# Blank tails issued four experts at a time, and fixed TensorE products at the seams between the stages, in a gated cross-attention and mixture-of-experts kernel

## The chip, the cores and the metric

The kernel is one program on one core of a Trainium2 chip. The metric is the device time of one execution in microseconds. Three runs of the kernel before gave 1041.34, 1044.93 and 1046.5 us, so the median is 1044.93 us.

## What is computed

The input x is 32 sequences of 256 tokens with 256 features, 8192 tokens in all. There are two residual steps, each gated by the tanh of a scalar.

```python
x = x + tanh(g_xattn) * xattn(layernorm(x), ctx)      # 8 heads of 64; ctx: 77 rows of 192 per sequence
x = x + tanh(g_ffn) * ffn(layernorm(x))

def ffn(xf):
    scores = softmax(xf @ Wg.T)                       # 16 experts
    wk, idx = top_k(scores, 2)
    cw = sum(one_hot(idx, 16) * wk[..., None], axis=1)
    h = gated_mlp_act(einsum('td,edh->teh', xf, W1))  # u * silu(g), 128 wide
    z = einsum('te,teh,ehd->td', cw, h, W2)
    return z + gated_mlp_act(xf @ Ws1) @ Ws2          # shared expert, 256 wide
```

## The kernel before

The work is four stages, one after the other. Each of the functions `prepare`, `attend`, `mix` and `passes` opens one block; a block ends for all engines together, when the last of them has come to its end, and the next opens then. Every float32 operand of a large product is split into a high and a low part in the type float32r, and three products (high-high, low-high, high-low; lines 75 to 77) stand for one.

`prepare` (line 284) loads and splits the weights, folds the query weights and the keys of the first four sequences into matrices M, and gathers layer-norm statistics of all 64 tiles of x on VectorE. The last key product on TensorE is that of `make_K` in line 385; VectorE closes the block with the steps of `rstd_steps` (lines 105 to 131).

`attend` (line 455) goes over the 32 sequences: scores, softmax, values, output projection, and the first residual, stored to a scratch tensor x1. It leaves the statistics of the second layer norm in `c.stats2`, a tile of 128 partitions and 384 columns that stays in place through the rest of the program. So does `c.ident`, the 128x128 identity.

`mix` (line 796) goes over 16 steps of 512 tokens: it normalises the rows, transposes them on TensorE (`transpose_y`, line 970), computes the router's logits (`score`), the shared expert, the two best experts of each token and the slot of each token in two lists sorted by expert, one for each choice. POOL scatters the rows to the DRAM tensor rows1, in the order of the experts of one choice. At the end four products (line 1045) bring a table into PSUM, from which the program reads where each tile of slots lies and which expert's weights it needs.

An expert's list seldom ends with a whole tile of 128 rows. `blank_tails` (line 1277) therefore writes 128 blank rows behind the last row of each expert, sixteen DMAs of 258 KB for each choice, issued on SyncE's queue; their places are loaded into SyncE's registers four at a time (line 1283). A blank row carries an index that makes a later scatter skip it.

`passes` (line 1289) goes over 40 pairs of tiles twice: the first pass reads rows1 and scatters to rows0, the second reads rows0 and scatters to the output. Its order is written out by hand:

- SyncE loads the rows of pair q into one of ten buffers (`load`, line 1335), two DMAs of 258 KB, and before that waits until the pair ten places earlier has been scattered from the same buffer. Between the loads of pairs 10 and 11 of the first pass it issues all sixteen blank tails of rows0 (line 1349). Before the second pass it waits for all scatters of the first and for the tails.
- TensorE does four things in each step (line 1429): the transposes of pair q, the up product of pair q-1 (`hidden`), the transposes of the activations of pair q-2, the down product of pair q-3. The weights of all experts lie in SBUF.
- ScalarE and VectorE take the results out of PSUM, VectorE adds the result to the row in place (line 1500), and POOL scatters the two tiles of a pair by indirect DMA (line 1364).

The places that the tails fill and the rows that the scatters write do not overlap.

Of the kernel before, what the change touches and what calls it, by code (L numbers as in the profile page):

```python
# [33 lines left out]
E, HID = 16, 128  # L34
# [201 lines left out]
def make_K(nc, pe, c, a, n, pair):  # L236
    wait(pe, a.M_lo, 4 * n)
    out, cols = a.ps_proj[1][:, 0:GK], slice(pair * P, (pair + 1) * P)
    products(nc, out, [(c.wk_hi[:, 0, cols], c.wk_lo[:, 0, cols], a.ctxM[0][:, 0, :], a.ctxM[1][:, :])], stop=False)
    stacked(nc, out, c.wk_hi[:, 1, cols], c.wk_lo[:, 1, cols], a.ctxM[0][:, 1, :]).then_inc(a.K_done, 1)  # L240
# [40 lines left out]
    low(nc, M_out(a, 1, parity, cc, h), M_out(a, 0, parity, cc, h), M_bank(a, cc), a.M_lo)  # L281


def prepare(nc, c, a):


# [2 lines left out]
    with ExitStack() as ctx:  # L289
        sb, _, sem = allocator(nc, ctx)  # L290
# [24 lines left out]
        with nc.Block() as block:  # L315
# [59 lines left out]
            @block.tensor  # L375
            def _(pe):
                pe.wait_ge(wk_lo_done, 1)
                pe.wait_ge(a.ctx_split, 1)
                for n in range(4):
                    make_K(nc, pe, c, a, n, n)  # L380
                    pe.wait_ge(wq_lo_done, 2)
                    for k in range(4):
                        make_M(nc, pe, c, a, n, n, k)
                pe.wait_ge(a.ctx_split, 2)
                make_K(nc, pe, c, a, 4, 0)

            @block.scalar
            def _(act):
# [407 lines left out]
def mix(nc, c):  # L796
# [6 lines left out]
    with ExitStack() as ctx:  # L803
# [11 lines left out]
        a = [sb(f"ca{i}", [P, 512]) for i in range(2)]  # L815
# [57 lines left out]
        with nc.Block() as block:  # L873
# [95 lines left out]
            def _(pe):  # L969
# [44 lines left out]
                def down(G):  # L1014
                    p = G % 2
                    pe.wait_ge(aT_lo, 2 * G + 2)
                    for b in range(2):
# [4 lines left out]
                                 ws2[0][:, n, :], ws2[1][:, n, :]) for n in range(2)])  # L1022
                        last.then_inc(o_done, 1)

                transpose_y(0)
                pe.wait_ge(wg_ready, 1)
                score(0)
# [17 lines left out]
                for n, column in enumerate((1, 0, 3, 2)):  # L1045
                    last = nc.tensor.matmul(ps_table[:, n * SLOT_TILES:(n + 1) * SLOT_TILES],
                                            table[0:SLOT_TILES, column:column + 1], c.ident[0:SLOT_TILES, 0:SLOT_TILES],
                                            start=True, stop=True)
                last.then_inc(table_rows, 1)

            @block.scalar
            def _(act):
# [236 lines left out]
def passes(nc, c):  # L1289
# [5 lines left out]
    with ExitStack() as ctx:  # L1295
# [35 lines left out]
        with nc.Block() as block:  # L1331

            @block.sync
            def _(sp):
                def load(dram, q):
                    u = q % U
                    wait(sp, scattered[u], 32 * (q // U))
                    with ExitStack() as registers:
                        held = [registers.enter_context(sp.register(f"rows_{q}_{i}")) for i in range(2)]
                        first = 2 * q  # L1340
                        sp.load(held, c.rows_at[0:1, first:first + 2])  # L1341
                        for i in range(2):
                            at = sp.snap(held[i], donate=True, min_val=0, max_val=ROWS - P)
                            sp.dma_start(row[u][:, i, :], dram[bass.ds(at, P), :]).then_inc(row_in[u], 16)  # L1344

                sp.wait_ge(c.blanked1, 16 * E)
                for q in range(PAIRS):
                    load(c.rows1, q)
                    if q == U:
                        blank_tails(nc, sp, nc.sync, c, c.rows0, 0, range(E), c.blanked0)  # L1350
                for u in range(U):
                    sp.wait_ge(scattered[u], 32 * ROUNDS)
                sp.wait_ge(c.blanked0, 16 * E)
                for q in range(PAIRS, 2 * PAIRS):
                    load(c.rows0, q)
# [21 lines left out]
            @block.tensor  # L1377
            def _(pe):


                def transpose_rows(q, u, j):
                    pe.wait_ge(row_in[u], 32 * (j + 1))
                    wait(pe, yT_lo, q - 1)
                    for i in range(2):
                        for k in range(DC):
                            last = nc.tensor.transpose(ps_y[u % 2][:, k, i * P:(i + 1) * P],  # L1386
                                                       row[u][:, i, YROW + k * P:YROW + (k + 1) * P], c.ident[:, :])
                    last.then_inc(yT_done, 1)

                def split(at, first):  # L1390

                    return (c.w_flat[:, bass.ds(at + first, D)], c.w_flat[:, bass.ds(at + (WHALF + first), D)])

                def hidden(q, p, at):
                    pe.wait_ge(yT_lo, q + 1)
                    wait(pe, a_done, 2 * (q - 1))
                    for i in range(2):
                        token = slice(i * P, (i + 1) * P)
                        last = products(nc, ps_h[p][:, i, :], [
                            (yT[p][0][:, k, token], yT[p][1][:, k, token], *split(at[i], k * D)) for k in range(DC)])  # L1400
                    last.then_inc(h_done, 1)

                def transpose_a(q, p):
                    pe.wait_ge(a_done, 2 * q + 2)
                    wait(pe, aT_lo, q - 1)
                    for i in range(2):
                        last = nc.tensor.transpose(ps_a[p][:, i, :], a[p][:, i, :], c.ident[:, :])  # L1407
                    last.then_inc(aT_done, 1)

                def down(q, p, at):  # L1410
                    pe.wait_ge(aT_lo, q + 1)
                    wait(pe, final, q - 1)
                    for i in range(2):
                        last = products(nc, ps_z[p][:, i, :], [
                            (aT[p][0][:, i, :], aT[p][1][:, i, :], *split(at[i], DC * D))])
                    last.then_inc(z_done, 1)

                def load_weights_at(known, q, u):


                    _, at = nc.values_load_multi_w_load_instructions(
                        c.weights_at[0:1, bass.ds(2 * q + 2, 4)], engines=[mybir.EngineType.PE], min_val=0,
                        max_val=(E - 1) * WROW, skip_runtime_bounds_check_because="the table is made of min(., E - 1)")
                    known[u], known[u + 1] = at[0:2], at[2:4]

                for first in (0, ROUNDS):
                    exists, known = inside(first), {}

                    def step(s, u, j):
                        if u == 0:  # L1430
                            known.clear()
                            if exists(s - 3):
                                load_weights_at(known, s - 3, -3)
                        if u % 2 == 0:
                            load_weights_at(known, s - 1, u - 1)
                        if exists(s):
                            transpose_rows(s, u, j)
                        if exists(s - 1):
                            hidden(s - 1, (u - 1) % 2, known[u - 1])
                        if exists(s - 2):  # L1440
                            transpose_a(s - 2, u % 2)
                        if exists(s - 3):
                            down(s - 3, (u - 3) % 2, known[u - 3])

                    rounds(pe, step, first, lag=3)
# [140 lines left out]
```

## Time and profile before

| | before |
|---|---|
| median of three runs | 1044.93 us |
| the profiled execution: its own time | 1043.86 us |
| its span in the trace | 1041.7 us |
| TensorE products, busy | 909.5 us (87%) |
| TensorE weight loads, busy | 857.2 us (82%) |
| VectorE, busy | 804.5 us (77%) |
| ScalarE, busy | 478.8 us (46%) |
| POOL, busy | 475.1 us (46%) |
| DMA traffic | 150.64 MB, mean 145 GB/s |
| mean granted TensorE clock | 0.956 of full speed |

The profile is that of one execution. Its page gives the busy time of each engine, and then the span in 40 slices of 26 us: a digit is the busy share of a slice in tenths, and the row of the clock gives the TensorE clock that was granted, 9 standing for 0.9 and more. The program's stages lie one after the other in these slices: `prepare` ends at 62 us, `attend` at 530, `mix` at 760; the second pass of `passes` begins near 908. [...] Before its first change in a trace the clock is printed as 1.00 whatever it is, so there the length of the products tells it.

### The profile page before, as it was taken

To read this page: it belongs to the slowest core of one execution; us is meant where nothing else is said; L and a number is where in the kernel's file an instruction comes from. 1 tells how busy PE (TensorE), PEld (TensorE's weight loads), DVE (VectorE), ACT (ScalarE), POOL (GpSimd) and SP (SyncE) were. 2 spreads that over 40 slices of the span, in tenths; PEclk is the share of its full clock that TensorE was granted. 3 is DMA by queue.
4 is the path that set the end of the run, shared out by engine and by line. 5 is a ranking of instruction groups with operands and counts; after the bars stand their busy time and mean duration, and the time that the engine had idled before them with its cause. 6 is when DMAs were issued, how large, how long until landed. Compare 5 with 4: busy or idle time off the path is not lost. (4 is left out here: it accounts for less than half of the span.)

```text
span 1041.7 us, 22369 instructions
## 1 busy us (share of the span) xinstructions
PE 909.5 (87%) x6728; PEld 857.2 (82%) x6729; DVE 804.5 (77%) x1837; ACT 478.8 (46%) x970; POOL 475.1 (46%) x495
## 2 busy tenths in 40 slices
PE   2559999999999999999949999999565899599994
PEld 2449999999999999998847888887465899499994
DVE  5768888888898888998737898888534677467773
ACT  3345555555555555554445455543122344144441
POOL 6134434343343434334321555455415466537775
PEclk9999999999999999999968999999868899889998
DMA  8621222122221222212151444442769899488890
GB/s 216 215 87 35 80 68 67 54 57 79 66 79 45 66 66 67 68 54 67 53 172 32 173 166 160 170 170 108 275 222 318 284 341 344 146 267 260 268 289 29
DMA packets 108096, 150.64 MB, mean 145 GB/s; under 512 B 21622, under 2 KB 72186, under 8 KB 108032
## 3 DMA queue, kind: packets, MB, share of 16 engines
q1 hardware_dynamic: 92672, 107.60, 34.1%
q0 software_dynamic: 15360, 42.24, 10.6%
q8 instruction: 35, 0.57, 0.2%
q14 instruction: 29, 0.24, 0.1%
HBM read 90.19 MB, written 65.90 MB: 150 GB/s over the span
## 5 line engine op out<-in xcount | busy, mean ns | idle before, releaser
L549 POOL TENSOR_TENSOR prob<-prob,row_sum 128x616 f32<-128x616 f32 x64 | 77.9, 1218 | 148.7 <-DVE row_sum L739 148.7
L1364 POOL DMA_INDIRECT rows_scratch<-prow x80 | 78.7, 983 | 75.0 <-DVE prow L1500 47.2
L956 POOL DMA_INDIRECT rows_scratch<-row,slot x64 | 67.8, 1060 | 75.8 <-DVE row L1203 61.2
L1364 POOL DMA_INDIRECT out<-prow x80 | 78.7, 983 | 50.1 <-issue 26.4
L1482 DVE TENSOR_TENSOR eyT_lo<-ps_ey,eyT_hi 128x512 fp32r<-128x512 f32 x80 | 55.2, 690 | 55.6 <-ACT eyT_hi L1457 55.1
L1457 ACT ACTIVATE eyT_hi<-ps_ey 128x512 fp32r<-128x512 f32 x80 | 47.9, 599 | 109.3 <-PE ps_ey L1386 109.3
L75 PE MATMUL ps_h<-w_flat,eyT_hi 128*128 x320 | 98.1, 307 | 0.0
L224 POOL TENSOR_TENSOR xT_lo<-xT_raw,xT_hi 128x512 fp32r<-128x512 f32 x32 | 41.2, 1286 | 121.7 <-ACT ctxb_hi L190 121.6
L1386 PE MATMUL ps_ey<-ident,prow 128*128 128x128 f32 x320 | 51.6, 286 | 49.2 <-DMA prow<-rows_scratch 45.9
L190 ACT ACTIVATE M_hi<-ps_proj 128x308 f32 (+1 forms) x128 | 54.4, 429 | 84.1 <-PE ps_proj L77 84.0
L76 PE MATMUL ps_h<-w_flat,eyT_hi 128*128 x320 | 90.9, 284 | 0.0
L77 PE MATMUL ps_h<-w_flat,eyT_lo 128*128 x320 | 90.7, 283 | 0.0
L75 PE MATMUL ps_s<-M_hi,xT_hi 128*128 (+1 forms) x256 | 81.4, 318 | 8.7 <-PEq L315 8.5
L1489 DVE SCALAR_TENSOR_TENSOR a<-ps_h,prow,silu 128x128 f32<-128x128 f32 x160 | 48.8, 347 | 47.8 <-ACT silu L1462 47.8
L195 DVE TENSOR_TENSOR PT_lo<-ps_pt,PT_hi 77x512 fp32r<-77x512 f32 x128 | 80.9, 671 | 0.3 <-ACT PT_hi L190 0.3
L1386 PEld LDWEIGHTS ps_ey<-ident,prow 128*128 128x128 f32 x320 | 38.5, 147 | 51.7 <-DMA prow<-rows_scratch 47.3
L76 PE MATMUL ps_s<-M_lo,xT_hi 128*128 (+1 forms) x256 | 78.6, 307 | 0.0
L77 PE MATMUL ps_s<-M_hi,xT_lo 128*128 (+1 forms) x256 | 78.6, 307 | 0.0
L75 PE MATMUL ps_o<-wo_hi,OT_hi 128*128 128x256 f32 x256 | 74.6, 291 | 1.4 <-DVE OT_lo L195 1.4
L75 PE MATMUL ps_o<-PT_hi,V_hi 96*128 96x256 f32 x256 | 72.9, 285 | 3.3 <-DVE PT_lo L195 3.3
L675 ACT ACTIVATE prob<-prob,rstd 128x616 f32<-128x616 f32 x64 | 52.0, 812 | 44.8 <-DVE prob L729 44.8
L76 PE MATMUL ps_o<-PT_lo,V_hi 96*128 96x256 f32 x256 | 72.4, 283 | 0.0
(232 smaller groups left out, 3383.3 us busy)
## 6 DMA issues: line engine op xcount, KB each, us to landing
prow<-rows_scratch SPq DMA_DIRECT2D x160, 258.0 KB, 3.8
rows_scratch<-blank SPq DMA_DIRECT2D x34, 258.0 KB, 4.0
xs<-in_x SPq DMA_DIRECT2D x16, 512.0 KB, 4.5
xT_raw<-in_xT SPq DMA_DIRECT2D x32, 256.0 KB, 3.8
x_tok<-in_x SPq DMA_DIRECT2D x32, 256.0 KB, 2.9
x_scratch<-x_tok SPq DMA_DIRECT2D x32, 256.0 KB, 3.0
row<-x_scratch SPq DMA_DIRECT2D x16, 512.0 KB, 4.0
w_raw<-in_W SPq DMA_DIRECT2D x16, 256.0 KB, 3.5
```

The lines of the kernel that those rows point to most:

```text
L75: nc.tensor.matmul(out, lh, rh, start=start and n == 0, stop=False)
L76: nc.tensor.matmul(out, lh, rl, start=False, stop=False)
L77: last = nc.tensor.matmul(out, ll, rh, start=False, stop=stop and n == len(pairs) - 1)
L190: nc.scalar.activation(out, source, ACT.Copy).then_inc(done, 1)
L195: nc.vector.tensor_tensor(lo, source, f32(hi), ALU.subtract).then_inc(done, 1)
L549: nc.gpsimd.tensor_tensor(pr, pr, row_sum[i][:, :].unsqueeze(2).broadcast_to((P, H, CK)), ALU.mult).then_inc(normed, 1)
L675: nc.scalar.activation(prob[i][:, :], prob[i][:, :], ACT.Exp, scale=c.rstd1[:, bass.ds(2 * b + i, 1)]).then_inc(exp_done, 1)
L956: pool.indirect_dma_start(c.rows1, bass.IndirectOffsetOnAxis(slot1[:, t:t + 1], 0), row[G % NX][:, i, :], None).then_inc(scattered[G % NX] ...
L1364: pool.indirect_dma_start(dram, bass.IndirectOffsetOnAxis(target, 0), row[u][:, i, 0:columns], None, bounds_check=bound, oob_is_err=False) ...
L1386: last = nc.tensor.transpose(ps_y[u % 2][:, k, i * P:(i + 1) * P], row[u][:, i, YROW + k * P:YROW + (k + 1) * P], c.ident[:, :])
L1482: V.tensor_tensor(yT[p][1][:, :, :], ps_y[p][:, :, :], f32(yT[p][0][:, :, :]), ALU.subtract).then_inc(yT_lo, 1)
L1489: V.scalar_tensor_tensor(a[p][:, i, :], ps_h[p][:, i, 0:HID], row[b][:, i, weight:weight + 1], silu[p][:, i, :], ALU.mult, ALU.mult).then_ ...
```

## The change

Four edits. After the last key product of `prepare`, TensorE does 24 products of the identity with itself. In `mix` it does ten products of the identity with the 384 columns of `c.stats2` ahead of the first transposes, and eighteen behind the table's products. In `passes` it does four such products at the opening of the first pass and eighteen ahead of the second. All are plain float32, go to a PSUM bank that is free at the time, wait for nothing, signal nothing and are read by nobody. And SyncE issues the blank tails of rows0 in groups of four experts, behind the loads of pairs 10, 16, 22 and 28, in place of all sixteen behind the load of pair 10.

```diff
@@ -281,6 +281,12 @@
     low(nc, M_out(a, 1, parity, cc, h), M_out(a, 0, parity, cc, h), M_bank(a, cc), a.M_lo)
 
 
+def busy(nc, c, bank, operand, count):
+
+    for _ in range(count):
+        nc.tensor.matmul(bank[:, 0:operand.shape[1]], c.ident[:, :], operand, start=True, stop=True)
+
+
 def prepare(nc, c, a):
 
 
@@ -383,6 +389,7 @@
                         make_M(nc, pe, c, a, n, n, k)
                 pe.wait_ge(a.ctx_split, 2)
                 make_K(nc, pe, c, a, 4, 0)
+                busy(nc, c, a.ps_proj[0], c.ident[:, :], 24)
 
             @block.scalar
             def _(act):
@@ -1022,6 +1029,7 @@
                                  ws2[0][:, n, :], ws2[1][:, n, :]) for n in range(2)])
                         last.then_inc(o_done, 1)
 
+                busy(nc, c, ps_h[0], c.stats2[:, :], 10)
                 transpose_y(0)
                 pe.wait_ge(wg_ready, 1)
                 score(0)
@@ -1047,6 +1055,7 @@
                                             table[0:SLOT_TILES, column:column + 1], c.ident[0:SLOT_TILES, 0:SLOT_TILES],
                                             start=True, stop=True)
                 last.then_inc(table_rows, 1)
+                busy(nc, c, ps_h[0], c.stats2[:, :], 18)
 
             @block.scalar
             def _(act):
@@ -1346,8 +1355,9 @@
                 sp.wait_ge(c.blanked1, 16 * E)
                 for q in range(PAIRS):
                     load(c.rows1, q)
-                    if q == U:
-                        blank_tails(nc, sp, nc.sync, c, c.rows0, 0, range(E), c.blanked0)
+                    first = (q - U) * 4 // 6
+                    if q >= U and (q - U) % 6 == 0 and first < E:
+                        blank_tails(nc, sp, nc.sync, c, c.rows0, 0, range(first, first + 4), c.blanked0)
                 for u in range(U):
                     sp.wait_ge(scattered[u], 32 * ROUNDS)
                 sp.wait_ge(c.blanked0, 16 * E)
@@ -1423,8 +1433,9 @@
                         max_val=(E - 1) * WROW, skip_runtime_bounds_check_because="the table is made of min(., E - 1)")
                     known[u], known[u + 1] = at[0:2], at[2:4]
 
-                for first in (0, ROUNDS):
+                for first, idle in ((0, 4), (ROUNDS, 18)):
                     exists, known = inside(first), {}
+                    busy(nc, c, ps_h[0][:, :, :].rearrange("p i h -> p (i h)"), c.stats2[:, :], idle)
 
                     def step(s, u, j):
                         if u == 0:
```

## Rows read from the trace of the kernel before

**Rows 1.** The page, part 2: TensorE's busy tenths and granted clock in 40 slices.
```profile
PE   2559999999999999999949999999565899599994
...
PEclk9999999999999999999968999999868899889998
```

**Rows 2.** Waits of TensorE from 764 to 1030 us: total, times, longest.
```profile
PE ps_ey L1386 <- DMA prow<-rows_scratch: 45.9, 5, 17.2
```

**Rows 3.** The chain that ended last, first pass: start, length (us), what.
```profile
784.07 0.31 SPq L1283
...
788.10 0.46 SPq L1283
...
810.46 1.12 PE ps_ey L1386 x4
...
814.73 0.44 PE ps_ey L1386 x4
...
848.92 0.44 PE ps_ey L1386 x4
...
851.67 0.44 PE ps_ey L1386 x4
```

**Rows 4.** Timeline of the first pass, SyncE's queue and one step of TensorE.
```profile
784.54 17.83 SPq L1286 DMA_DIRECT2D rows_scratch<-blank  x16
...
850.60 11.57 SPq L1344 DMA_DIRECT2D prow<-rows_scratch  x9
...
856.99 0.60 PE L1386 MATMUL ps_ey<-ident,prow 128*128 128x128 f32 x4
```

**Rows 5.** The page, part 6: DMA issues, median us to landing at the end.
```profile
prow<-rows_scratch SPq DMA_DIRECT2D x160, 258.0 KB, 3.8
```

**Rows 6.** Waits of SyncE's queue from 820 to 890 us: total, times, longest.
```profile
SPq L1341 <- DMA rows_scratch<-prow: 28.1, 20, 6.8
```

**Rows 7.** Windows of the first pass; last three columns: granted clock, DMA share, GB/s.
```profile
784.00:890.00 106.00, 88.94 (x761) 88.22 (x760) 69.61 (x160) 39.59 (x94) 62.24 (x64) 0.94 0.96 328
...
786.00:798.00 12.00, 9.29 (x80) 8.92 (x78) 8.22 (x19) 4.42 (x11) 7.86 (x8) 1.00 1.04 367
...
840.00:880.00 40.00, 39.16 (x342) 38.99 (x342) 30.73 (x71) 18.06 (x44) 27.04 (x28) 1.00 0.99 341
```

**Rows 8.** Timeline of TensorE at the passes' starts; brackets: idle before, its releaser.
```profile
746.29 0.71 PE L1046 MATMUL ps_r<-ident,table 80*1 80x80 f32 x8
...
764.20 1.11 PE L1386 MATMUL ps_ey<-ident,prow 128*128 128x128 f32 x4 [17.19 <-DMA prow<-rows_scratch]
...
767.04 0.56 PE L75 MATMUL ps_h<-w_flat,eyT_hi 128*128 x1
...
911.28 1.12 PE L1386 MATMUL ps_ey<-ident,prow 128*128 128x128 f32 x4 [12.37 <-DMA prow<-rows_scratch]
```

**Rows 9.** Timeline from the end of `prepare` into `attend`.
```profile
53.95 0.46 PE L85 MATMUL ps_proj<-ctxM_hi,wk_lo 128*128 128x308 f32 x1
...
62.95 0.60 PE L75 MATMUL ps_s<-M_hi,xT_hi 128*128 128x308 f32 x1 [8.54 <-PEq L315]
...
66.17 0.46 PE L75 MATMUL ps_proj<-kT_hi,wq_hi 128*128 128x308 f32 x1
...
69.23 0.30 PE L76 MATMUL ps_s<-M_lo,xT_hi 128*128 128x308 f32 x1
```

**Rows 10.** Timeline from the opening of `mix` to its first transposes.
```profile
530.84 0.27 DVE L117 TENSOR_TENSOR mean<-stats 128x64 f32<-128x64 f32 x1 [2.22 <-PEq L504]
...
538.32 1.97 PE L975 MATMUL ps_cy<-ident,row 128*128 128x128 f32 x8 [10.62 <-ACT row L1084]
```

**Rows 11.** The chain at the opening of `passes`: SyncE's first register load.
```profile
760.01 0.47 SPq L1341
```

**Rows 12.** Windows in which the clock rises again; columns as in rows 7.
```profile
772.00:774.00 2.00, 2.00 (x18) 2.00 (x17) 0.76 (x4) 1.01 (x3) 0.00 (x0) 0.93 1.03 322
...
918.00:920.00 2.00, 2.00 (x15) 2.00 (x15) 1.04 (x3) 0.60 (x1) 0.00 (x0) 0.73 1.01 346
```

## The prediction

> **What bounds the kernel now.** I read the page first. Its slices show a TensorE that is nine tenths busy nearly everywhere, with dips at four places, and at these places, or just behind them, the granted clock drops too [rows 1]. [...] Then the waits of TensorE alone over the expert passes: 45.9 us go to rows that had not landed, in five waits [rows 2]. Three are the starts of the two passes; one is inside the first pass, and the chain says why: SyncE issues a burst of blank tails (line 1286), and the eleventh pair's rows come behind it [rows 3]. Last the timeline at the four seams between stages, read below: they hold 8.54, 10.62, 17.19 and 12.37 us without a product.
>
> **The tails.** The sixteen DMAs take the queue from 784.54 to 802.37; TensorE has ten pairs of rows in hand, uses them up and stands still until 810.46. The step from pair to pair is 2.75 us in the steady state (848.92 to 851.67), so the pair that starts at 810.46 would have started 14.2 us earlier: the idle stretch, 14.15 us by the timeline, is lost whole. The next pair follows after 4.27 us (810.46 to 814.73, counted to its transposes) in place of 2.75, since the clock has fallen: another 1.5. The stall costs 15.7 us [rows 3, 4].
>
> What comes back? The change issues the same sixteen DMAs, four behind each of the loads 10, 16, 22 and 28. One group of four held SyncE for 4.0 us (784.07 to 788.10). In the steady state the ring has little to lend: the ninefold issue row begins at 850.60 with the load that TensorE uses at 856.99; landing takes 3.8 us in the median from the issue of the second half some 0.5 us later, so 2 us are spare [rows 4, 5]. SyncE itself waits for scatters (28.1 us in 20 waits over 25 pairs), 1.1 us per pair, and can catch up in that [rows 6]. By the queue alone the first group is free (six or more us in hand there), and each later one costs 0 to 2 us: 0 to 6.
>
> The DMA engines are the harder limit. From 784 to 890 they moved 328 GB/s over 106 us, 34.8 MB, and all of it stays. With 15.7 us less they would have to carry 34.8 MB in 90.3 us, 385 GB/s. The steady stretch moves 341 at a busy share of 0.99, the crowded 786 to 798 moves 367 at 1.04 [rows 7]. At 341 GB/s the stretch takes 102.0 us, which gives back 11.7; at 367 it takes 94.8 and gives back 4.5; at 385 nothing. I take 6 us, near the row with all three kinds of transfer in it, which is the mix that the change makes. Net of the tails: 15.7 - 6 = 9.7 us, bounds 4 and 15.7. [...]
>
> **The fixed products.** Each is an identity times 128 or 384 columns of plain float32. The nearest row is the table product of line 1046: four calls are eight records of 80 columns, and the eight start within 0.48 us (0.71 less the last's 0.23), 0.069 apart [rows 8]. [...] A call of 384 columns is then 0.64 us at the full clock and 1.28 at half, one of 128 columns 0.21 and 0.43. None signals anybody; each delays only what follows on TensorE, and the end of its block.
>
> Seam A (24 of 128 columns): from 54.4, where the last key product ends, to 62.95, where attention opens after VectorE's chain [rows 9]. 5.1 us at full clock, 10.2 at half. The products run at half clock until 69.2 (the first one of 0.30 us in place of 0.46 is at 69.23), 6.2 us after dense work begins; if the burst raises the clock as this dense work did, it needs at most 6.2 + 2 = 8.2 us and ends in time. Gain: the twelve score products that open the stage, 62.95 to 66.17, shrink by 1.6 us, and the softmax chain that the first transposes wait for starts that much earlier. Taken 1.5; bounds 2 late and 3 early.
>
> Seam B (10 of 384): the block opens at 530.8, rows are ready for transposes at 538.32 [rows 10]. 6.4 us at full clock, 12.8 at half; the clock is low at the start, so 8 to 10 us, which ends 0.5 to 2.5 us late. It then speeds the transposes and the scores behind them, and the clock may drop in the waits between. Taken 1; bounds -3 and 3.
>
> Seam C (18 behind the tables, 4 at the opening of the passes): from 747.0, the clock being full, 11.5 us to 758.5; SyncE's first load of the passes is at 760.01, so the block's end isn't delayed; four more take 2.6 us and end ahead of the rows at 764.20. Without them the clock stayed low until the slice 772 to 774 (0.93), some 8 us, 5 of them dense; that is worth 2.6 us at most [rows 8, 11, 12]. A quiet stretch before the rows come lets the clock fall again, so I take 1.5; bounds -2 and 3.
>
> Seam D (18): 898.9 + 11.5 = 910.4, just ahead of 911.28. The low clock lasted into the slice 918 to 920 (0.73): again 1.5, bounds -1 and 3 [rows 8, 12].
>
> **Sum.** 9.7 + 1.5 + 1 + 1.5 + 1.5 = 15.2 us. The profiled execution took 1043.86 us (span 1041.7 and 2.2 around it); 1028.7 by it. The median of the runs is 1.1 us above that execution: 1029.8, said as 1029.5.
>
> **The rivals.**
> R1, the engines have room: short stretches carry the 385 GB/s. Nothing comes back, 15.7, and the seams give 5.5 to 8: 1021 to 1024. For it speaks that shares above 1 occur; against, the steady rows at 0.99 with 341. 0.12.
> R2, the seams give nothing: the wait for rows behind each burst drops the clock again before dense work begins. For it: at C and D the first pair's transposes stand alone for 2 us before the second pair lands. [...] As a mechanism here it takes B, C and D to zero and leaves A: 9.7 + 1.5, so 1033.7. 0.18.
> R3, the tails' stall is split, not removed: each group holds the queue its 4.0 us with no slack left, 16 us for four against 15.7. Only the seams count: about 1039.5. Against it are the 2 us in the ring and SyncE's own idle time. 0.12.
> R4, slower: plain float32 identity products do not keep or raise the clock. Then the bursts run at half clock: A 10.2 us ends at 64.6 (1.7 late), B 12.8 at 543.6 (5.3 late), C 23 at 770.0 and the four on top at 775 (11 late), D 23 at 921.9 (10.6 late), 28.6 late in all; less 9.7, 19 us slower, 1064. It decides from the point where C and D run at half clock for over 5 us each. Against it: at C and D the clock is full when the burst begins. 0.07.
>
> **How the numbers follow.** Forecast 0.51, R1 0.12, R2 0.18, R3 0.12, R4 0.07. The range 1021 to 1039 holds the first three and half of R3. About 0.5% (5 us) is what a measurement of this kernel can tell from no change, the runs before spread by as much; so below 1039.7 is faster: forecast, R1, R2 and half of R3, 0.87. The other half of R3 is the same, 0.06, and R4 slower, 0.07.
>
> **What would show it.** No wait of 14 us inside the first pass; in its place a few of 1 to 3 us behind loads 16, 22 and 28, each with a line 1286 ahead of it, and the DMA share at 1.0 until the pass ends. The first pass's steady step still 2.75. Fixed products 0.64 us apart at C and D with the granted clock at 1.00 between 747 and 759. The score products at 63 to 66 some 0.13 apart, not 0.26. I am wrong if the stretch of the pass is shorter by under 5 or over 14 us, or if a seam's first real product comes more than 2 us later than now.

## The result

The changed kernel takes **1039.16 us** (median of six runs, 1034.72 to 1041.35) against 1045.89 of the kernel before in the same comparison (six runs, 1041.34 to 1047.29). The ratio is 0.9933, 95% interval 0.9906 to 0.996: 6.7 us faster, between 4.2 and 9.8. The forecast was 15.2 us faster, so more than half of the gain isn't there. The profiled execution took 1040.25 us, 3.6 less than that of before; what is read between the two traces below has to add up to 3.6, and can't account for the other 3 us of the medians.

The page of the kernel after, TensorE's busy tenths, its clock and the DMA engines' busy tenths in 40 slices, then the landing time of rows; to be held against [rows 1] and [rows 5]:

```profile
PE   2579999999999999999968999999889789999994
PEclk9989999999999999999998999999999898999997
DMA  7631221222221222112142444443869999388890
...
prow<-rows_scratch SPq DMA_DIRECT2D x160, 258.0 KB, 3.8
```

The dips of TensorE at the seams are mostly filled, as they must be: the fixed products count as busy. In the first pass the clock shows two dips (slices 32 and 34) in place of the one long dip of [rows 1] (slices 31 and 32). That is the place to look. TensorE's waits for rows from 784 to 890 us in the kernel after (total, times, longest):

```profile
PE ps_ey L1396 <- DMA prow<-rows_scratch: 11.2, 4, 4.9
```

In the kernel before it was one wait of 14.15 us. So nothing of 14 us is left, as foretold, but four waits hold 11.2 us, and the clock makes up the rest. The timeline of TensorE around the second of them, with the transposes of six pairs in turn:

```profile
806.38 0.60 PE L1396 MATMUL ps_ey<-ident,prow 128*128 128x128 f32 x4
809.13 0.60 PE L1396 MATMUL ps_ey<-ident,prow 128*128 128x128 f32 x4
816.92 1.11 PE L1396 MATMUL ps_ey<-ident,prow 128*128 128x128 f32 x4 [4.89 <-DMA prow<-rows_scratch]
822.10 0.87 PE L1396 MATMUL ps_ey<-ident,prow 128*128 128x128 f32 x4
825.12 0.60 PE L1396 MATMUL ps_ey<-ident,prow 128*128 128x128 f32 x4
```

The steps are 2.75, 7.79, 5.18 and 3.02 us. After an idle stretch of only 4.89 us the transposes take 1.11 in place of 0.60, and the step behind it is almost double: the granted clock, 1.00 before, is 0.50 from 815.8 to 822.7. (All the clock records of the twenty traces of this case read 1.00 or 0.50; what lies between is the mean of a window. That is the "full" and "half" of the prediction.) That costs 2.4 us on top of the wait. The fourth group brings the same again: a wait of 4.28 us at 858.17, the clock at 0.50 from 856.8 to 863.6, then a step of 5.19. Windows of the kernel after (PE, PEld, VectorE, ScalarE, GpSimd busy, then granted clock, DMA share, GB/s):

```profile
784.00:887.00 103.00, 90.84 (x739) 89.57 (x738) 67.95 (x155) 38.83 (x93) 60.71 (x62) 0.93 0.96 334
...
792.00:804.00 12.00, 10.22 (x90) 9.90 (x88) 7.78 (x19) 4.43 (x11) 6.80 (x7) 1.00 1.04 391
812.00:817.00 5.00, 0.11 (x2) 0.08 (x2) 1.18 (x3) 0.00 (x0) 3.26 (x4) 0.88 1.04 401
817.00:823.00 6.00, 6.00 (x30) 6.00 (x31) 2.30 (x5) 1.33 (x3) 0.00 (x0) 0.53 1.03 374
866.00:872.00 6.00, 6.00 (x55) 6.00 (x54) 4.83 (x12) 2.76 (x7) 3.94 (x5) 1.00 0.68 201
```

While TensorE stands still (812 to 817) the DMA engines are full, a share of 1.04 at 401 GB/s: the rows that it waits for are issued and under way. Later the engines run part empty (866 to 872, 0.68): a load waits for the scatter of the pair that held its buffer, and TensorE has fallen behind with that pair. SyncE's waits from 862 to 876 us:

```profile
SPq L1350 <- DMA rows_scratch<-prow: 8.8, 3, 4.0
```

So the high rates of a few microseconds aren't kept: over 103 us it is 334 GB/s.

What a group of four can do shows in the chain that ended last, in the kernel after, at the second group:

```profile
801.15 0.31 SPq L1292
...
801.97 0.36 SPq L1295
...
803.92 1.02 SPq L1295
...
805.00 1.11 SPq L1350
...
806.27 0.35 SPq L1353
...
806.81 10.07 DMA prow<-rows_scratch
816.92 1.11 PE ps_ey L1396 x4
```

From the register load (line 1292) to the next load of rows (line 1353) the group holds SyncE about 5 us, of which some 2.5 are a delay: the last packet of the scatter that freed the buffer landed at 802.9. Then the rows take 10.07 us to land, counted from the issue of the pair's second half. The 3.8 us of [rows 5] is no measure for that: it is a median over both passes. Where the trace tells the landing of a load, it took, in the kernel before from 784 to 890 us and from 914 to the end, and in the kernel after from 784 to 890:

```profile
DMA to landing us min/median/max: 3.7/4.6/6.3
DMA to landing us min/median/max: 2.6/3.4/4.3
DMA to landing us min/median/max: 3.2/5.5/7.0
```

Without tails in the stretch (e5 below) the second halves alone take 5.0 us in the median. Against that the landing at this group is 5 us late and the queue 2.5; at the fourth group (7.87 us to land, the buffer free at 843.9, the load issued at 849.7) it is nearly 3 us each. Both have a share, and the landing's is not the smaller one.

To compare stages I use the starts of the transposes of pairs 0, 4, 10, 39 and 40, and like marks at the other stages (us, one profiled execution each; "e7" and the like are experiments below). "Attention" goes from its first score product to the last product ahead of `mix`.

| stretch | before | after | e7 tails alone | e8 products alone | e5 tails last | e6 last + products |
|---|---|---|---|---|---|---|
| start to first score product | 62.9 | 64.3 | 63.2 | 64.2 | 63.3 | 63.7 |
| attention | 464.8 | 466.6 | 464.7 | 465.6 | 465.6 | 466.3 |
| its end to first transposes of `mix` | 10.6 | 10.6 | 10.8 | 12.5 | 10.6 | 12.6 |
| from there to the end of the table product | 208.7 | 205.0 | 208.6 | 206.0 | 208.7 | 206.1 |
| from there to pair 0 | 17.2 | 17.6 | 17.7 | 17.2 | 17.7 | 17.2 |
| pair 0 to pair 4 | 11.5 | 9.2 | 11.1 | 10.3 | 11.2 | 10.2 |
| pair 4 to pair 10 | 17.6 | 17.1 | 17.4 | 17.3 | 16.9 | 17.1 |
| **pair 10 to pair 39** | **97.7** | **97.7** | **95.7** | **100.0** | **83.7** | **83.3** |
| pair 39 to pair 40 | 20.2 | 20.2 | 20.3 | 20.7 | 21.2 | 22.0 |
| pair 40 to the end of TensorE's last product | 116.4 | 115.8 | 115.5 | 115.6 | 116.4 | 115.5 |

The bold row is where the tails stand, and it hasn't moved at all. 29 steps of 2.75 us would be 79.8; both kernels lose 18 us there. Between these two traces the gain of 3.6 us comes from `mix` (3.7) and the opening of the first pass (2.3), with half a microsecond each from pairs 4 to 10 and from the second pass, less what the start of attention, attention itself and the way to pair 0 lose (3.6). The rows ahead of the passes have to be read with care: over the twenty traces of this case attention takes 464.1 to 468.1 us, 464.1 to 466.6 in the six with products ahead of it and 464.7 to 468.1 in the fourteen without, so that the 1.8 us that it "loses" here tell nothing.

### The profile page after: what moved, and what is told of

The parts are those of the page before. It is cut to its first block and busy times, and to the rows that moved or that the text cites. A ratio compares the mean times of both kernels' runs of the same rounds, so it can differ in the third digit from the quotient of the medians.

```text
span 1038.1 us, 22665 instructions
## 1 busy us (share of the span) xinstructions
PE 945.8 (91%) x6876; PEld 879.8 (85%) x6877; DVE 803.0 (77%) x1837; ACT 479.2 (46%) x970; POOL 475.6 (46%) x495
## 5 line engine op out<-in xcount | busy, mean ns | idle before, releaser
L963 POOL DMA_INDIRECT rows_scratch<-row,slot x64 | 67.8, 1059 | 76.5 <-DVE row L1212 61.8
L77 PE MATMUL ps_o<-PT_hi,V_lo 96*128 96x256 f32 x256 | 73.0, 285 | 0.0
L76 PE MATMUL ps_o<-wo_lo,OT_hi 128*128 128x256 f32 x256 | 71.9, 281 | 0.0
```

What stands on the lines that cost most here:

```text
L76: nc.tensor.matmul(out, lh, rl, start=False, stop=False)
L77: last = nc.tensor.matmul(out, ll, rh, start=False, stop=stop and n == len(pairs) - 1)
L963: pool.indirect_dma_start(c.rows1, bass.IndirectOffsetOnAxis(slot1[:, t:t + 1], 0), row[G % NX][:, i, :], None).then_inc(scattered[G % NX] ...
```

## The experiments

Two theories of the measured gain at first: **A**, the stall comes back (the third rival), and what is gained are the seams; **B**, the tails give most of it and the seams nothing or less. For the stall there were in turn two causes: the **bytes** of the tails, which share full engines with the rows, or SyncE's **queue**, held by a register load and four issues. The kernel before is run beside every kernel; a ratio is to it, on the same chip.

### The halves, and the tails in another stage

e1: the kernel after without any fixed product. e2: only the products, the tails where the kernel before has them. e3: no products, and all sixteen tails moved ahead of the passes, behind the other sixteen in `mix`. e4: e3 with the products.

```diff
 e1, e3 (every call of busy goes)
-                busy(nc, c, ps_h[0], c.stats2[:, :], 18)
 e2
-                    first = (q - U) * 4 // 6
-                    if q >= U and (q - U) % 6 == 0 and first < E:
+                    if q == U:
-                        blank_tails(..., range(first, first + 4), c.blanked0)
+                        blank_tails(..., range(E), c.blanked0)
 e3, e4
                 blank_tails(nc, sp, nc.sync, c, c.rows1, 1, range(E), c.blanked1)
+                blank_tails(nc, sp, nc.sync, c, c.rows0, 0, range(E), c.blanked0)
```

> The tails in groups of four, no fixed products. Theory 1 (crowded ring: a group of four in DMA engines that are already full delays the rows behind it and the scatters beside it, and the ring of ten buffers has only some 2 us to lend): the first pass gains nothing clear, 0 to 3 us, so 1043 to 1046; two or three stalls of 2 to 5 us stay in the trace. Rival (the forecast's term of 9.7 us holds and the fixed products cost what is missing): 1035 to 1038.

> The fixed products, the sixteen tails in one piece as before. Theory 1: nearly the whole of the measured gain is theirs, 4 to 8 us, so 1038 to 1042, and the first pass keeps its one stall of 14 us. Rival: the products gain nothing or lose, 1044 to 1048.

> No fixed products, and the tails of the second pass issued in the stage before, right behind those of the first, where TensorE is idle and the DMA engines run empty from 754 on. Theory 1: the first pass runs without a stall at 2.75 us per pair, and the stage before ends no later, since its end waits for POOL's drain at 759.8: 15 to 17 us less, 1028 to 1031. Rival (the DMA engines cannot carry rows and scatters at that step either, so that stalls stay): 5 to 10 less. Second rival (the sixteen DMAs push the last scatters and the end of the stage back): 8 to 12 less, with the first load of the passes 4 us or more later.

> The tails as in the run before this one, with the fixed products of the change. If the two parts add up: the gain of the tails in the stage before plus that of the products alone, 1021 to 1025. If the products only win where a stall left the clock low: no better than the run without them.

Measured: e1 0.9947 (0.992 to 0.9974), e2 1.001 (0.9985 to 1.0035), e3 0.9983 (0.9961 to 1.0005), e4 0.9942 (0.992 to 0.9964). On this chip, though, the kernel before took 1104.5 us, 59 more than in the comparison that gave the result, so none of the times foretold can be held against it, and the traces show why the ratios can't be carried over either. Both passes go at about 3.6 us per pair in place of 2.75; the stages ahead of them are as long as ever. TensorE's waits in e18, a later run on such a chip, from 800 to 870 us:

```profile
PE ps_h L75 <- DVE eyT_lo L1489: 9.8, 8, 1.5
PE ps_ey L1392 <- issue: 3.4, 4, 1.6
```

It never waits for rows there, but for VectorE and its own instructions: ScalarE and VectorE both fall silent together, for 3.3 and 2.7 us, every 7.3 us or so (806 to 828). The DMA engines have room in such a pass, a share of 0.84 in e18 from 800 to 870, so it can't show what tails cost where rows are the limit.

It shows the other side, what fours do where there is room. From 784 to 900 us e1's share of the DMA engines is 0.92, and TensorE never waits for rows there. e2, with the sixteen in one piece, still has the stall (its waits from 784 to 905 us):

```profile
PE ps_ey L1395 <- DMA prow<-rows_scratch: 9.7, 1, 9.7
```

Its pairs 10 to 39 take 114.9 us, e1's 107.3; in the twelve traces of slower passes that have tails one by one, behind the last load or in `mix`, they take 102.9 to 107.1. So here the stall does go when it is split, as the forecast had it for the faster passes. (e2 has the fixed products and e1 not, but none of them stands in this stretch.) e4 is 5.0 us below e3 by the medians, with intervals that barely overlap, while the products of e2 give nothing.

e3 is no gain, for the reason that its second rival gave. SyncE's queue in e3:

```profile
733.00 27.36 SPq L1293 DMA_DIRECT2D rows_scratch<-blank  x32
766.23 5.49 SPq L1351 DMA_DIRECT2D prow<-rows_scratch  x8
```

Thirty-two tails hold it to 760.4. GpSimd's scatters of `mix` share the engines with them (a DMA share of 1.01 from 733 to 760, 0.74 in e1), its drain behind the last one starts at 760.04 in place of 755.81 (e1), and the first load of the passes goes out at 766.23 in place of 762.05. From the table product to pair 0 e3 takes 22.3 us, e1 17.3.

### Tails behind the last load, and the halves again

On a chip where the kernel before takes 1042.81 us (19 runs; e5 and e6 have four runs each, e7 and e8 ten). e5: no products; all sixteen tails behind the first pass's last load, when SyncE has nothing else to fetch. e6: e5 with the products. e7 and e8 are e1 and e2 again.

```diff
 e5, e6
                 for q in range(PAIRS):
                     load(c.rows1, q)
-                    first = (q - U) * 4 // 6
-                    if q >= U and (q - U) % 6 == 0 and first < E:
-                        blank_tails(..., range(first, first + 4), c.blanked0)
+                blank_tails(nc, sp, nc.sync, c, c.rows0, 0, range(E), c.blanked0)
```

> No fixed products; all sixteen tails behind the last load of the first pass, where SyncE has nothing to do for some 20 us and the DMA engines are half empty and then empty. Theory 1 (the tails' cost lies in delaying rows and scatters in full DMA engines): the first pass runs through at 2.75 us per pair with no wait for rows after the opening, its span shrinks by 15 to 17 us, and the second pass starts no later behind it: 1028 to 1031 where the kernel before takes 1044 to 1046. Rival (the DMA engines cannot carry rows and scatters alone at that step, so waits appear anyway): 5 to 10 us less only. On a chip of the kind of the first batch, where both passes run at some 3.6 us per pair, rows are no limit and the gain shrinks to 5 to 12.

> As the run before this one, with the change's fixed products. Theory 1 and products that give 2 to 6 us at the seams: 1023 to 1027. Rival (the products give nothing on top): within 1.5 us of the run without them.

> The change's tails in groups of four, no products, once more, in case the chip is one that runs the passes at 2.75 us per pair: theory 1: 0 to 4 us less than before (1041 to 1046), with two or three stalls in the first pass whose idle time and low clock together cost 12 to 18 us. Rival (forecast): 8 to 12 less.

> The fixed products, tails in one piece, once more. Theory 1: 3 to 6 us less than before (1039 to 1042). Rival, as the first batch had it: no difference, 0 to 1 us.

| kernel | median us | ratio | 95% |
|---|---|---|---|
| e5 | 1031.33 | 0.9886 | 0.9857 to 0.9915 |
| e6 | 1028.99 | 0.9853 | 0.9825 to 0.988 |
| e7 | 1039.82 | 0.9964 | 0.9949 to 0.998 |
| e8 | 1042.29 | 0.9998 | 0.9979 to 1.0017 |

e5 settles that the price of the tails lies in their standing inside the full stretch. From pair 10 to pair 39 it takes 83.7 us in place of 97.7: **14.0 us**, against the 15.7 that I had counted for the stall. On its own chip the same step out of the stretch is worth 12.0 us from fours (e7 to e5) and 16.7 from one piece (e8 to e6). By the medians e5 is 11.5 us below the kernel before, just above the 1028 to 1031 that was expected. TensorE's waits for rows in e5 from 784 to 890 us:

```profile
PE ps_ey L1391 <- DMA prow<-rows_scratch: 1.8, 2, 0.9
```

Its windows, columns as above:

```profile
784.00:876.00 92.00, 88.36 (x767) 87.51 (x767) 69.78 (x160) 40.10 (x96) 62.64 (x65) 1.00 0.97 332
872.00:890.00 18.00, 13.61 (x110) 12.59 (x108) 11.43 (x26) 5.05 (x13) 12.56 (x14) 0.98 1.04 368
```

And its queue:

```profile
784.39 87.22 SPq L1350 DMA_DIRECT2D prow<-rows_scratch  x60
872.12 17.69 SPq L1292 DMA_DIRECT2D rows_scratch<-blank  x16
895.43 3.97 SPq L1350 DMA_DIRECT2D prow<-rows_scratch  x6
```

The tails take SyncE 17.7 us, as in [rows 4], but now TensorE has the last ten pairs in hand. The price is 1.0 us at the change of passes (21.2 against 20.2). The clock stays at 1.00 until 876 and the engines' share at 0.97: without the tails the DMA engines are still nearly full, and the two waits of 1.8 us in all show how little is spare.

e7 says what spreading in fours does by itself: two waits, 8.3 us in all, where e5 has 1.8, and the step from pair 10 to pair 39 is only 2.0 us shorter than in the kernel before. Its chain ahead of the first of them:

```profile
795.96 5.76 DMA rows_scratch<-prow
801.74 0.95 SPq L1347
...
804.60 0.36 SPq L1292
...
809.03 0.35 SPq L1350
809.57 7.90 DMA prow<-rows_scratch
817.52 1.11 PE ps_ey L1393 x4
```

Here the load ahead of the group has to wait for a scatter (5.76 us), then comes the group, then a load that lands in 7.90. So the pattern of the kernel after isn't its products' doing. At the medians e7 is 3.0 us below the kernel before, inside the 0 to 4 of its theory. e8: the products alone are worth nothing that this can measure (0.9998, 2 us either way), as its rival had it, though the table shows 2.7 us won in `mix` and 1.2 at the opening of the first pass; 1.9 us of later first transposes, 2.1 of a later and longer attention, and a longer pass 10 to 39 (100.0, with the one stall of 15.2 us) stand against it in that trace. On top of e5 they bring 2.3 us more (e6), with intervals that overlap: not shown, and neither what its theory nor what its rival said. e6 is the fastest kernel seen here, 13.8 us below the kernel before by the medians, 15.3 by the ratio (12.5 to 18.2). That is about what I had forecast for the change, but by other sums: its tails give 11.5 where I had 9.7, its products 2.3 where I had 5.5.

So neither theory of the gain is shown. By the two profiled executions the seams gave all of it and the stretch nothing; by the halves on this chip the tails in fours gave 3.0 us (0.2 to 0.5%, clear of zero) and the products nothing clear. The halves together make less than the 6.7 us of the whole change on its own chip.

### Bytes or queue

e10: no products, the tails one at a time behind every second load from the eleventh pair's on. e11: tails behind the last load as in e5, but in the change's four places SyncE still loads four registers and issues four DMAs of 16 bytes a row to a place that nobody reads: the queue's time without the bytes. e9 and e12: e6 with the products only in `mix`'s end and the passes' openings, and e5 with only the 24 products that end `prepare`.

```diff
 e10
-                    first = (q - U) * 4 // 6
-                    if q >= U and (q - U) % 6 == 0 and first < E:
-                        blank_tails(..., range(first, first + 4), c.blanked0)
+                    first = (q - U) // 2 if q % 2 == 0 else E - 1
+                    if q >= U and (q % 2 == 0 or q == PAIRS - 1):
+                        blank_tails(..., range(first, first + 1), c.blanked0)
 e11
-                        blank_tails(..., range(first, first + 4), c.blanked0)
+                        narrow_blanks(nc, sp, c, c.nowhere, first, c.blanked0)
+                blank_tails(nc, sp, nc.sync, c, c.rows0, 0, range(E), c.blanked0)
...
+        eng.load(held, c.tails[0:1, first:first + 4])
+        for i in range(4):
+            nc.sync.dma_start(dram[at:at + P, 2 * D:ROW], c.blank[:, 2 * D:ROW]).then_inc(done, 16)
 e9 (of e6)
-                busy(nc, c, a.ps_proj[0], c.ident[:, :], 24)
...
-                busy(nc, c, ps_h[0], c.stats2[:, :], 10)
 e12 (of e5)
+                busy(nc, c, a.ps_proj[0], c.ident[:, :], 24)
```

> All tails behind the last load, and fixed products only around the passes (18 behind the tables, 4 and 18 at the passes' openings), none in the two earlier seams. If those two seams cost as much as they give (what the traces so far show: the attention stage not shorter, the transposes of the next stage 1.9 us late against 2.6 us gained behind them), this is no slower than tails last with all products, and 1.5 to 4 us faster than tails last alone: 1026 to 1030. Rival (the earlier seams give): 1 to 3 us slower than with all.

> No products; the sixteen tails inside the first pass one at a time, behind every second load from the tenth on. If what hurts is four in a row, each single tail (0.7 us of the DMA engines) is lent by the ring, and most of the 14 us that leaving the tails out of the pass gives is had: 1032 to 1036. Rival (the DMA engines are full, so the sixteen cost their own time wherever in the full stretch they stand, some 11 us): 1039 to 1043.

> Tails last, no products; in the change's four places SyncE loads four registers and issues four DMAs as there, but each writes 16 bytes a row in place of 2064, to a tensor that nobody reads. If the bytes in the full DMA engines are what stalls the pass: the time of tails last alone, within 2 us (1030 to 1033). If SyncE's time at the issue is (four DMAs and a register load, 2.5 to 4 us in front of the next load): the stalls come back, 6 to 12 us slower than tails last.

> All tails behind the last load, and only the 24 products at the end of the first stage. If they give nothing: within 1 us of tails last alone, the attention stage again 464.7 to 466.5 us long and opened 0.3 to 1 us later. Rival (my step A): 1 to 3 us faster than tails last alone.

The chip was again one of the slower passes (the kernel before 1099.8 us), so the questions that the expectations put were not answered: e9 0.992 (0.9891 to 0.995), e10 0.9939 (0.9914 to 0.9964), e11 0.9941 (0.9915 to 0.9967), e12 0.9955 (0.9928 to 0.9983). e10 and e11 differ from each other by nothing, and from e12 by nothing that the intervals part. e10, e11 and e9 were run twice more, for a chip on which rows are the limit (e13 and e16 are e10, e14 and e17 are e11, e15 and e18 are e9, without a changed line):

> One tail behind every second load, no products, once more, for a chip that runs the passes at 2.75 us per pair. If what hurts is four in a row: most of the 14 us, 1032 to 1036. Rival (the DMA engines are full, the sixteen cost their own 11 us wherever they stand in the full stretch): 1039 to 1043.

> Tails last, and in the change's four places register loads and DMAs of 16 bytes a row, once more. If the bytes stall the pass: within 2 us of tails last alone (1030 to 1033). If SyncE's time at the issue does: 6 to 12 us slower than tails last.

> Tails last, products only around the passes, once more. If the earlier two seams pay for nothing: 1027 to 1030, no slower than tails last with all products (1029.0 where the kernel before takes 1042.8). Rival: 1 to 3 us slower than that.

> One tail behind every second load, no products, a third time, since both tries fell on chips that run the passes at some 3.6 us per pair. At 2.75 us per pair: 1032 to 1036 if four in a row is what hurts, 1039 to 1043 if the sixteen cost their own time wherever they stand in the full stretch. At 3.6 us per pair: again 0.3 to 0.8% less than before, which tells nothing of the two.

> Tails last with narrow groups in the change's places, a third time. At 2.75 us per pair: within 2 us of tails last (1.1% less than before) if the bytes stall the pass; 0.2 to 0.6% less than before if SyncE's time at the issue does. At 3.6 us per pair: again 0.4 to 0.8% less than before.

> Tails last, products only around the passes, a third time. At 2.75 us per pair: 1.2 to 1.7% less than before if the two earlier seams pay for nothing, 1.0 to 1.2% if they give. At 3.6 us per pair: again 0.6 to 1.1% less.

| | first | second | third |
|---|---|---|---|
| kernel before, us | 1099.82 | 1104.08 | 1099.99 |
| one by one (e10, e13, e16) | 0.9939 | 0.9944 | 0.993 |
| narrow groups (e11, e14, e17) | 0.9941 | 0.994 | 0.9922 |
| last, products at the passes (e9, e15, e18) | 0.992 | 0.9913 | 0.993 |

Both times the slower passes came again. In a window of e11 where three of its groups fall, the DMA share is 0.87; the question needs it near 1. Columns as above:

```profile
800.00:870.00 70.00, 58.23 (x476) 54.91 (x475) 42.90 (x97) 23.36 (x58) 37.44 (x39) 1.00 0.87 272
```

All nine intervals end below 1 (the highest at 0.9967), so on such chips too each of the three is worth 0.6 to 0.9%; more these runs don't tell apart. **Bytes or queue stays open as an experiment.** What speaks for the bytes is the trace and a sum. At the second group a load that was late by 2.5 us in the queue took 5 us longer to land than such loads do in e5. And sixteen tails of 258 KB are 4.2 MB, 12.7 us at the 334 GB/s of the stretch, of the 14.0 us that e5 wins by taking them out of it. What speaks for the queue is that it was late by 2.5 to 3 us at each of the two groups that TensorE waited longest behind. Neither is proof.

## Why the prediction failed, step by step

**The reading of the stall was right.** I had 15.7 us for it, and e5, which takes the tails away from the full stretch, wins 14.0 us there and 11.5 at the median.

**"What comes back" is the step that failed.** Of the 15.7 us, 15.7 came back in the kernel after and 13.7 in e7, by the bold row; my own sign of being wrong, a stretch shorter by under 5 us, is there. I took 6 us, between 4.5 at 367 GB/s and 11.7 at 341, because the crowded 12 us of [rows 7] had the mix of transfers that the change makes. A rate over 12 us isn't one over 100. The kernel after does reach 391 and 401 in short windows; but each stall that they end in leaves the engines part empty later (201 GB/s from 866 to 872), since loads wait for scatters and those for TensorE. Over the stretch it is 334. In my own formula, 34.8 MB at 334 GB/s are 104.2 us, and of 15.7 come back 13.9; what's left is 1.8, and the two traces with the tails in fours show 0 and 2.0. That sum is bookkeeping, since the rate is read from the very stretch whose length it gives; it says that the formula was sound and its rate wrong, not why the rate is what it is. [Rows 7] had 328 GB/s over 106 us with the stall in it, at a share of 0.96 already; e5, which hardly waits for rows, has 332 at 0.97. The bound at the steady row was still too hopeful, and the middle was the wrong end.

**The queue's own bound was also too kind**, 0 to 6 us with 2 us spare. The slack was worked out with rows that land in 3.8 us, the median over both passes. In the very stretch the kernel before's landed in 4.6 in the median, which leaves 1 us spare and not 2, before any tail is added. Behind a group they landed in 10.07, 7.87 and 7.90 us, so the slack is gone before the queue's delay is counted. The first group I called free; a wait of 1.78 us stood behind it. I foretold "a few of 1 to 3 us", and got 4.89 and 4.28, with the clock at 0.50 behind both. That price I had charged to the one stall and not to its parts: 2.4 us each, 5 in all. These 5 and the 11.2 us of waits are the 16 us of the third rival. Its total, 1039.5, stands beside 1039.16, just outside the range (1021 to 1039); but that is partly luck, for it has the seams give 5.5 us, which they did not. Its mechanism was half right: at the two long waits the queue was late by 2.5 to 3 us, and the landing by 5 and 3.

**Prices of the products: right.** The fixed products behind the tables and before pass two, timeline of the kernel after:

```profile
746.51 11.88 PE L287 MATMUL ps_ch<-stats,ident 128*128 128x384 f32 x36
...
895.89 11.77 PE L287 MATMUL ps_h<-stats,ident 128*128 128x384 f32 x36
...
908.34 0.66 PE L1396 MATMUL ps_ey<-ident,prow 128*128 128x128 f32 x4 [0.68 <-DMA prow<-rows_scratch]
```

36 records in 11.88 us are 18 calls of 0.64 us (11.5) and the tail of the last, ending at 758.4 (758.5 was said) and 907.7. The granted clock was 1.00 from 746 to 759 and from 896 to 908, so no plain float32 product ran at half clock there. The row of 0.069 us for 80 columns would by proportion give 0.66 a call and not 0.64; what I reckoned with is what the runs show. A call is two records in the trace. One of 384 columns takes 0.32 us from start to start at a clock of 1.00 and 0.64 at 0.50 (e8, 533 to 538), so a call 0.64 and 1.28; one of 128 columns takes 0.21 before the clock's rise at 58.1 and 0.11 behind it in the kernel after, a call 0.43 and 0.21. The fourth rival is out.

**Seam A: wrong.** 1.5 us said, nothing gained. TensorE in the kernel after from the burst on:

```profile
55.80 5.94 PE L287 MATMUL ps_proj<-ident 128*128 128x128 f32 x42
64.33 0.38 PE L75 MATMUL ps_s<-M_hi,xT_hi 128*128 128x308 f32 x1 [2.60 <-PEq L321]
...
66.30 0.46 PE L75 MATMUL ps_s<-M_hi,xT_hi 128*128 128x308 f32 x1
...
69.53 0.31 PE L75 MATMUL ps_s<-M_hi,xT_hi 128*128 128x308 f32 x1
```

The burst raised the clock, in fact: it rose at 58.1 (first rise at 56.9 to 58.9 in the six traces with these products, at 66.4 to 69.6 in the fourteen without). The burst ended at 61.7, TensorE stood for 2.60 us, and half a microsecond after the stage opened, at 64.9, the clock fell to 0.50, until 68.3: the score products have 0.46 us each, as before. I had written that it "ends in time" and held the clock for won. That VectorE's chain, and with it attention, also starts later here (64.3 against 62.95; 64.2 in e8) was no part of my sum; over all traces that is 63.5 to 64.3 in the six with these products and 61.8 to 64.2 in the fourteen without, so a price of theirs is not shown.

**Seam B: right in kind, low in size.** Said 1 us. In `mix` the kernel after is 3.7 us shorter (2.7 in e8 and 2.6 in e6), and its products met the clock at 1.00 (534.2 to 540.2):

```profile
534.10 6.69 PE L287 MATMUL ps_ch<-stats,ident 128*128 128x384 f32 x20 [3.14 <-PEq L511]
541.56 1.09 PE L982 MATMUL ps_cy<-ident,row 128*128 128x128 f32 x8 [0.77 <-ACT row L1093]
```

In e8 and e6 it was not so: the clock was 0.50 until 538.7 and 539.0, the same burst took 9.57 and 9.61 us and the transposes came 1.9 and 2.0 later, as my "0.5 to 2.5" had it. The net is then under 1 us. The gain behind the transposes is real: from them to the end of the table product it is 205.0 to 206.3 us in the five traces with these products, and 207.3 to 209.0 in the fifteen without.

**Seam C: right.** 2.3 us from pair 0 to pair 4 (1.5 said), 1.2 in e8; the rows were there 1.24 us after the last product, and the clock was still at 1.00. Over all traces pairs 0 to 4 take 8.6 to 10.5 us with these products and 10.2 to 11.9 without. **Seam D:** 1.5 said, some 0.5 found (11.0 against 11.5 from pair 40 to 44). Here the second rival's mechanism has its place: waits of 0.68 and 2.01 us for rows follow the burst, and the clock was at 0.50 again from 911.4 to 914.8 in the kernel after. At seam C the waits were 1.24 and 1.76, and it stayed at 1.00; in e8 they were 1.32 and 1.45, and it was 0.50 from 767.4 to 770.8. In the slower passes seam D gave more: with the tails last, pairs 40 to 44 took 8.7 to 9.3 us (e9, e15, e18) against 11.4 without products (e12). Together the seams made between 0 (e8, medians) and 3 us (the profiled executions), not 5.5.

## What to carry to other kernels

DMAs that are spread through a stretch where the engines' busy share is already near 1 (0.96 in the kernels before and after) can cost there what they cost in one piece (97.7 us both ways here, 95.7 in e7); where there was room (0.92 in e1) the stall went. Divide by the rate of the whole stretch, not by that of its fullest 12 us, take landing times from the stretch too, and move such DMAs to where the ring has nothing more to fetch (here behind the pass's last load, worth 11.5 us). A stall split into pieces can pay for the clock at each of them, as the waits of 4.28 and 4.89 us did here, 2.4 us each. Products that fill a seam are worth only what dense work finds of their clock: in the kernel after the waits of 1.24 and 1.76 us that followed them at the first pass left it at 1.00, the 2.60 us at attention did not, and in e8 it fell to 0.50 at the first pass too; try them one seam at a time.

## What was not expected

- Chips differ. On two kinds of chip the kernel before takes about 1043 or 1100 us, the first 750 us being alike and both passes 2.75 or about 3.6 us a pair. In the slower ones ScalarE and VectorE fall silent together, for 3.3 and 2.7 us every 7.3 us in e18. The cause wasn't found, and a change whose effect hangs on a limit has to be tried on the kind of chip where the limit is met.
- A load of 258 KB lands in 3.8 us in the median of both passes, in 4.6 in the full stretch of the kernel before, and in up to 10.07 behind a group of four of the same size.
- The granted clock fell to 0.50 half a microsecond after dense work had begun (64.9 us), having been raised by the products ahead of it.
- `prepare` ends at times that differ between traces by more than the fixed products in it can be seen to do. The last statistics of VectorE in `prepare` start at 58.1 to 58.9 us in the six traces with products there, and at 56.4 to 58.8 in the fourteen without.
